# One of the seven products of a gate/up pair made by seven smaller ones over half the tokens

## The chip, the cores and the metric

The kernel runs on one core of one Trainium2 chip. Its time is the device time of one launch in microseconds (us): 1729.62 us before the change, the median of three runs (1728.55 to 1730.23). The matrix engine is TensorE (PE in the profile, PEld its weight loads). VectorE is DVE, ScalarE is ACT, GpSimd is POOL, SyncE is SP; SP issues nearly all the transfers (DMAs). PE accumulates in eight PSUM banks `ps[0]` to `ps[7]`, each of 128 partitions by 512 float32.

## The reference

The input `x` is 64 batches of 64 rows (4096 tokens) by 1024. A small network on `cond_128` gives each batch a 64x64 matrix and a bias, and `y = A x + bias`. Then a feed-forward layer with ternary weights, 1024 to 2752 and back, is added to `x`:

```python
def _bitlinear(x, w):
    scale = jnp.mean(jnp.abs(w))
    q = jnp.round(jnp.clip(w / (scale + EPS), -1.0, 1.0))
    return x @ (q * scale).T

gate = _bitlinear(y, w_gate)
up = _bitlinear(y, w_up)
out = x + _bitlinear(gate * up, w_down)
```

## The kernel before

The tokens go in eight chunks of 512. Chunk 0 quantises and transposes the weights and is computed plainly. Chunks 1 to 7 work on pairs: a pair is two 128-feature tiles of gate and the two of up; there are ten pairs (`NPR`) and half a pair left over (pair 10). Activations are float32 and are split into a float16 high part and a float16 rest, so each weight tile meets two matmuls; weights are fp8.

For each pair the product of a 2x2 block matrix is made by seven products instead of eight (Winograd's form of Strassen's method): the 1024 inputs and the 512 tokens are halved, and so are the four feature tiles of the pair. Products `P1` to `P7` take sums of weight blocks, made once in chunk 0 and kept in device memory (`wcomb`), and sums of activation quarters, made on DVE for each chunk. Each product is 16 matmuls of 128x128 weights by 256 tokens (`product`, L881): two feature tiles (gate and up, side by side in one bank), four inputs tiles, two float16 parts. Gate times up is taken on DVE, and two groups of products (`down_group`, L938) multiply back to 1024, one in the middle of the chunk, after pair 5, and one at its end; DVE adds their results to the output (`output2`, L1762).

Every engine runs its own program in the order in which the code is written; semaphores tie them. In pair `p` PE makes P1, P2, then P4 of the pair before, then (in pairs 2 to 9) one eighth of the next chunk's `y` (`conv`, L658), P6, P5, P3 of the pair before, P7. ACT copies P1 (`copy_p1`, L1241), P1+P6 (`copy_p16`, L1248) and P1+P6+P7 (`copy_p167`, L1255) out of the banks, and in pairs 0 and 1, right behind `copy_p1`, copies the chunk's input to where the output grows (`residual`, L1043, four 128x1024 copies). DVE adds P2, P5 and P3 to those copies (`c11`, `c22`, `c12`), multiplies gate by up (`i11` and so on) and makes the sums of the result.

SP's program for a chunk is one list. `next_x` waits for the chunk's four residual copies, then loads the next chunk's 2 MB of `x` into `xa` and its bias into `bbc`; `pairs` loads each pair's weights from pair 3 on into a ring of three (`ring_load`); `next_pairs` loads the first three pairs of the next chunk, `store2` stores the output, and `down_load` loads the weights of a down group. A step that waits holds back all that stands behind it in the list. From chunk 2 on the chunks run in a loop (`Fori`), the last chunk is written out again.

Of the kernel before, what the change touches and what calls it, by code (L numbers as in the profile page):

```python
# [5 lines left out]
def adaln_ternary_ffn(nc: bass.Bass, x, cond, w0, b0, w1, b1, w2, b2, wk, bias_k, w_gate, w_up, w_down, out):  # L6
# [108 lines left out]
    AFTER = {"P6": "P1", "P7": "P6", "P4": "P7", "P2": "P4", "P3": "P5"}  # L115
    OUT = {"P1": (0, 0), "P2": (0, 0), "P6": (0, 1), "P3": (0, 1), "P4": (2, 0), "P7": (2, 1), "P5": (2, 1), "D": (2, 1)}
    BLOCK = {"P1": 0, "P6": 1, "P5": 2, "P2": 3, "P7": 4, "P4": 5, "P3": 6}

# [41 lines left out]
    with ctx:  # L160
# [27 lines left out]
        scl = bbc  # L188
        raw5 = sb("raw5", [P, CT], f32)

        msk = sb("msk", [P, NM, CT], f8)
# [178 lines left out]
        def wd_block(p, b):  # L370
            at = (p % GRP) * PART + b * BLK
            return wd_flat[:, at:at + BLK]

        psb = [p[:, :].bitcast(bf16) for p in ps]
# [104 lines left out]
        s_wst = [sem("s_wst0"), sem("s_wst1")]  # L479
        s_ring = [sem(f"s_ring{i}") for i in range(RING)]  # L480
        s_turn_pe, s_turn_pool, s_turn_sp = sem("s_turn_pe"), sem("s_turn_pool"), sem("s_turn_sp")
        s_st = [sem(f"s_st{t}") for t in range(NT)]
# [8 lines left out]
        def _(sp):  # L491
# [56 lines left out]
            def ring_load(p):  # L548
# [4 lines left out]
                else:  # L553
                    sp.dma_start(wg_flat[:, at:at + PART].bitcast(f32), wcomb[p, 0]).then_inc(s_ring[p % RING], 16)

            def next_pairs(c):
                for p, before in ((0, NPR - 1), (1, NPR), (2, NPR - 2)):
                    sp.wait_ge(s_m3, NS * (c - FIRST) + before + 1)
                    ring_load(p)

            def down_load(g):
# [3 lines left out]
            def pairs(c):  # L565
                for p in range(RING, NS):
                    sp.wait_ge(s_m3, NS * (c - FIRST) + p - RING + 1)
                    ring_load(p)
# [47 lines left out]
        def _(pool):  # L616
# [28 lines left out]
            for j, i in enumerate(ITEMS):  # L645
# [3 lines left out]
                nc.gpsimd.dma_start(dst, stage(j).bitcast(f32)).then_inc(s_wst[j % 2], 16)  # L649
            chunk(1)  # L650
            with pool.Fori(2, NC - 1) as c:
                chunk(c)
# [3 lines left out]
        def _(pe):  # L656
# [175 lines left out]

            def product(c, p, what):
# [4 lines left out]
                if what == "P1":  # L838
                    pe.wait_ge(s_ring[p % RING], 16 * ((4, 4, 3)[p % RING] * (c - FIRST) + p // RING + 1))
# [31 lines left out]
                elif what == "P3":  # L871
                    pe.wait_ge(s_c22, n + 1)
                if p == 0:
                    pe.wait_ge(s_ylo, KH * c + OPERAND[what] + 1)
                waited(c)
                for h in range(2 if p < NPR else 1):
# [7 lines left out]
                last.then_inc(s_done[what], 1)  # L884

# [17 lines left out]
            def down_group(c, g, more):  # L903
                n, done = NS * (c - FIRST), DN * FIRST + ND2 * (c - FIRST) + g * len(DOWN[0])
                for d, (what, j) in enumerate(DOWN[g]):
                    bank = DBANK[g][CHAIN[what]][j]
                    if d == 0:
                        pe.wait_ge(s_wd, 16 * (2 * (c - FIRST) + g + 1))
                        pe.wait_ge(s_loA, NPR * (c - FIRST) + g * GRP + GRP - 1)
                        pe.wait_ge(s_loS, NPR * (c - FIRST) + g * GRP + GRP - 1)  # L910
                        if g:
                            pe.wait_ge(s_i21, n + NPR)
                    if what in AFTER:
                        pe.wait_ge(s_o, done + DOWN[g].index((AFTER[what], j)) + 1)
                    elif what == "P1" and j:
                        pe.wait_ge(s_c11, n + (NS if g else GRP + 1))
                    elif what == "P5" and g == 0:
                        pe.wait_ge(s_c12 if j else s_i21, n + GRP)
                    elif what == "P5" and j == 0:
                        pe.wait_ge(s_c12, n + NPR)  # L920
                    elif what == "P5":
                        pe.wait_ge(s_uvr, c - FIRST + 1)
                    elif what == "D":
                        pe.wait_ge(s_c12 if j else s_i21, n + NS)
                        if j == 0:
                            pe.wait_ge(s_ulo, UP * FIRST + 2 * (c - FIRST) + 2)
# [64 lines left out]
            def pairs(c, more):  # L991
                for p in range(NS):
                    if p == GRP + 1:
                        down_group(c, 0, more)
                    product(c, p, "P1")
                    product(c, p, "P2")
# [23 lines left out]
        def _(act):  # L1020
# [186 lines left out]
            def hi_quarters(c):  # L1207
                act.wait_ge(s_ysc, KH * c + KH)
                for s in range(8):
                    hi_quarter(c, s)  # L1210

# [57 lines left out]
            def hi_sums(c, p):  # L1269
                act.wait_ge(s_sums, 4 * (NPR * (c - FIRST) + p) + 4)  # L1270
                nc.scalar.copy(pair_parts(p, 0, 3, 4), sums).then_inc(s_hiS, 1)  # L1271

            def hi_rest(c):
                act.wait_ge(s_wr, c - FIRST + 1)
# [5 lines left out]
            def pairs(c, more):  # L1280
                for p in range(NS):
                    copy_p1(c, p)
# [26 lines left out]
        def _(dve):  # L1309
# [291 lines left out]
            def sum_quarter(c, s):  # L1601
# [11 lines left out]
                else:  # L1613
                    dve.wait_ge(s_sy, 4 * (c - FIRST) + 3)
                    dve.wait_ge(s_ylo, KH * c + A12 + 1)
                    V.tensor_tensor(quarter(S4), quarter(A12), quarter(S2), ALU.subtract).then_inc(s_sy, 1)

# [47 lines left out]
            def c11(c, p):  # L1665
# [5 lines left out]
                elif p:  # L1671
                    dve.wait_ge(s_i22, NPR * (c - FIRST) + p)
                elif later(c):
# [15 lines left out]
            def c22(c, p):  # L1689
                n, w = NS * (c - FIRST) + p, width(p)  # L1690
                dve.wait_ge(s_m5, n + 1)
                dve.wait_ge(s_q67, n + 1)
                if p:
                    dve.wait_ge(s_i12, NPR * (c - FIRST) + p)
# [8 lines left out]
            def c12(c, p):  # L1703
                n, w = NS * (c - FIRST) + p, width(p)
                dve.wait_ge(s_m3, n + 1)
                dve.wait_ge(s_q6, n + 1)
                if p < NPR - 1:
                    dve.wait_ge(s_i11, NPR * (c - FIRST) + p + 2)
# [4 lines left out]
            def i12(c, p):  # L1713
                dve.wait_ge(s_c12, NS * (c - FIRST) + p + 1)
                V.scalar_tensor_tensor(a_block(p, A12), rr[:, u], PROD, rr[:, g], ALU.mult, ALU.mult).then_inc(s_i12, 1)  # L1715

            def i21(c, p):
                dve.wait_ge(s_m4, NS * (c - FIRST) + p + 1)
# [3 lines left out]
            def sums3(c, p):  # L1722
                m = NPR * (c - FIRST) + p
                dve.wait_ge(s_i21, NS * (c - FIRST) + p + 1)
                if p or later(c):
                    dve.wait_ge(s_loS, m)
# [38 lines left out]
            def tail(c, more):  # L1765
                lo_a(c, NPR - 1)
                c22(c, NPR)
                lo_s(c, NPR - 1)
                if more:
                    scales(c + 1)  # L1770
                dve.wait_ge(s_gr, c + 1)
# [16 lines left out]
                        (("scale", 6), ("scale", 7)), (("sum", S1), ("lo", A11)), (("lo", A21),), (("sum", S3),), \  # L1788
                        (("sum", S2),), (), (("lo", A12),), (("sum", S4),), (("lo", A22),), (("lo", S1),), (("lo", S2),), \
                        (("lo", S3),), (("lo", S4),)  # L1790
                for d in range(len(DOWN[1])):
                    output2(c, 1, d)
                    if more:
                        for what, k in steps[d]:
                            if what == "scale":
                                scale_y(c + 1, k)
                            elif what == "sum":
                                sum_quarter(c + 1, k)
# [8 lines left out]
            def pairs(c, more):  # L1807
                for p in range(NS):
# [10 lines left out]
                    if p < NPR:  # L1819
                        c11(c, p)  # L1820
# [6 lines left out]
                    if more and p - 2 in range(KH):  # L1827
                        conv(c + 1, p - 2)
                    if p:
                        c12(c, p - 1)  # L1830
                        i12(c, p - 1)
                        sum4(c, p - 1)
                tail(c, more)

# [30 lines left out]
```

## Time and profile before

| | |
|---|---|
| median of three runs | 1729.62 us |
| the profiled execution's own span, first to last instruction | 1726.1 us |
| PE busy, share of the span | 1707.7 us, 99% |
| matmuls of the products (L881) | 8232 |
| matmuls of the down groups (L938) | 1960 |
| DVE, ACT, POOL busy | 63%, 33%, 2% |
| mean granted TensorE clock, share of full speed | 0.999 |

A timeline row has the start and length in us from the span's start. Matmuls are pipelined, so the records of two that follow each other overlap: the pace of PE is read from the distance of starts, not from the length of a record. What an engine waited for stands in brackets behind a row, with the us that it was idle. An engine that is far from full can still hold PE up, if PE waits for one of its steps; how full it is on average doesn't tell that.

### The profile page before, as it was taken

What the parts mean: (1) busy time and instruction counts of PE and PEld (TensorE: products, weight loads), DVE (VectorE), ACT (ScalarE), POOL (GpSimd) and SP (SyncE); (2) the same over time, 40 slices, a digit from 0 to 9 for tenths busy, and PEclk for the clock granted to TensorE, in tenths of its full rate; (3) what the DMA queues carried; (4) which work ended last, traced back from release to release, by engine and by line L of the source; (5) the groups of instructions that cost most, each with busy time, mean ns of one, the idle gap of its engine ahead of it and who ended that gap; (6) DMA issues with size and microseconds to landing.
All of it is one profiled execution on the core that took longest, in us unless ns stands there. A gap on an engine that the chain in (4) does not pass through costs nothing.

```text
span 1726.1 us, 31355 instructions
## 1 busy us (share of the span) xinstructions
PE 1707.7 (99%) x12424; PEld 1215.6 (70%) x12424; DVE 1096.0 (63%) x1786; ACT 575.6 (33%) x921; POOL 28.0 (2%) x59
## 2 busy tenths in 40 slices
PE   6999999999999999999999999999999999999999
PEld 5554545968769596795958768596776959678684
DVE  6898895555766468554685646755576545855464
ACT  6887732312333133230333213231233313323120
POOL 0010000000000000000000000000000000000000
PEclk9999999999999999999999999999999999999999
DMA  8666626312242032420224211331223313132021
GB/s 342 249 229 239 221 96 219 121 44 97 76 148 96 22 108 77 168 66 22 107 102 164 65 75 54 129 137 43 97 76 126 101 40 108 65 124 79 29 87 49
DMA packets 59735, 194.06 MB, mean 112 GB/s; under 512 B 5280, under 2 KB 5600, under 8 KB 59584
## 3 DMA queue, kind: packets, MB, share of 16 engines
q1 hardware_dynamic: 56432, 177.49, 28.9%
q0 software_dynamic: 2560, 14.36, 2.2%
q8 instruction: 109, 1.79, 0.4%
q14 instruction: 42, 0.34, 0.1%
q10 hardware_dynamic: 592, 0.09, 0.0%
HBM read 160.90 MB, written 31.01 MB: 111 GB/s over the span
## 4 chain that ended last, share of the span: by engine, by line
PE 97%; DVE 2%; DMA 1%; issue 0%; ACT 0%; SPq 0%; DVEq 0%
PE ps L881 52%; PE ps L938 25%; PE ps L658 17%; PE ps L899 2%; PE ps L761 1%; DMA xa<-in_x_dram 1%; DVE wsum L1318 0%; DVE ys L1413 0%; DVE msk L1458 0%; DVE ys L1380 0%; DVE xa L1529 0%; DVE prod L1496 0%; DVE yp L1418 0%; ACT wdT L1106 0%; SPq L493 0%
## 5 line engine op out<-in xcount | busy, mean ns | idle before, releaser
L881 PE MATMUL ps<-yp,wgT 128*128 128x256 f16 x4116 | 902.4, 273 | 1.1 <-issue 1.1
L881 PE MATMUL ps<-wuT,wgT 128*128 128x256 f16 x4116 | 902.4, 273 | 0.0
L881 PEld LDWEIGHTS ps<-yp,wgT 128*128 128x128 fp8e4 x4116 | 402.9, 98 | 50.8 <-issue 2.9
L881 PEld LDWEIGHTS ps<-wuT,wgT 128*128 128x128 fp8e4 x4116 | 402.7, 98 | 48.3
L938 PE MATMUL ps<-wdT,inter 128*128 128x512 fp8e4 x1960 | 433.2, 379 | 0.0
L938 PEld LDWEIGHTS ps<-wdT,inter 128*128 128x128 f16 x1960 | 191.1, 98 | 227.2 <-issue 1.4
L1762 DVE SCALAR_TENSOR_TENSOR xr<-ps,osc,xr 128x512 f32<-128x512 f32 x210 | 156.4, 748 | 168.2 <-PE ps L938 128.4
L1711 DVE TENSOR_TENSOR wdT<-ps,msk 128x512 f32<-128x512 f32 (+1 forms) x77 | 51.3, 666 | 207.1 <-PE ps L881 207.1
L1241 ACT COPY raw<-ps 128x512 f32<-128x512 f32 (+1 forms) x77 | 43.7, 567 | 314.6 <-PE ps L881 314.0
L1248 ACT COPY msk<-ps 128x512 f32<-128x512 f32 (+1 forms) x77 | 43.6, 567 | 138.1 <-PE ps L881 138.1
L1263 ACT COPY inter<-ps 128x256 f32<-128x256 f32 x70 | 26.1, 372 | 180.1 <-PE ps L881 180.1
L1745 DVE TENSOR_TENSOR inter<-inter 128x1024 f16<-128x1024 f32 x70 | 85.3, 1218 | 0.0
L1205 ACT CAST yp<-ys 128x1024 f16<-128x1024 f32 x49 | 48.5, 1042 | 102.0 <-DVE ys L1413 59.0
L1675 DVE TENSOR_TENSOR wdT<-ps,raw 128x512 f32<-128x512 f32 x70 | 48.4, 692 | 43.7 <-PE ps L881 43.1
L658 PE MATMUL ps<-yp,wgT 128*128 128x512 f16 x336 | 76.1, 379 | 0.0
L658 PE MATMUL ps<-yp,wuT 128*128 128x512 f16 x336 | 75.1, 379 | 0.0
L658 PE MATMUL ps<-wdT,inter 128*128 128x512 fp8e4 x336 | 73.8, 379 | 0.0
L1267 ACT CAST inter<-prod 128x768 f16<-128x768 f32 x35 | 29.1, 832 | 132.7 <-DVE prod L1715 132.7
L1271 ACT CAST inter<-inter 128x1024 f16<-128x1024 f32 x70 | 73.3, 1047 | 0.0
L1267 ACT CAST inter<-wuT 128x768 f16<-128x768 f32 x35 | 29.1, 832 | 127.7 <-DVE wuT L1715 127.7
L1697 DVE TENSOR_TENSOR wdT<-ps,raw 128x512 f32<-128x512 f32 (+1 forms) x77 | 50.8, 660 | 32.4 <-ACT raw L1255 32.4
L658 PE MATMUL ps<-ablk,xa 128*128 128x128 f32 x512 | 69.5, 282 | 0.6 <-DMA xa<-in_x_dram 0.3
(229 smaller groups left out, 1497.9 us busy)
## 6 DMA issues: line engine op xcount, KB each, us to landing
wgT<-wcomb SPq DMA_DIRECT2D x70, 896.0 KB, 4.7
wdT<-dcomb SPq DMA_DIRECT2D x14, 2240.0 KB, 10.9
xa<-in_x_dram SPq DMA_DIRECT2D x8, 2048.0 KB, 7.8
out_dram<-xr SPq DMA_DIRECT2D x64, 256.0 KB, 2.0
wcomb<-xa POOLq DMA_DIRECT2D x17, 448.0 KB, 3.0
xr<-in_L_ffn_w_down_dram SPq DMA_DIRECT2D x9, 512.0 KB, 5.5
inter<-in_L_ffn_w_gate_dram SPq DMA_DIRECT2D x7, 512.0 KB, 16.6
wdT<-in_L_ffn_w_up_dram SPq DMA_DIRECT2D x7, 512.0 KB, 4.4
```

What stands on the lines that cost most here:

```text
L658: return nc.tensor.matmul(o, l, r, start=start, stop=stop)
L881: last = nc.tensor.matmul(out, w, operand(i, OPERAND[what])[:, k, :], start=(start and h + k + i == 0), stop=(k == KQ - 1 and i == 1), ski ...
L938: last = nc.tensor.matmul(bank[:, :], x, wd_block(p, BLOCK[what]), start=(what in ("P1", "P2", "P5") and q + i == 0), stop=(q == GRP - 1 a ...
L1205: nc.scalar.copy(operand(0, s), quarter(s)).then_inc(s_yhi, 1)
L1241: nc.scalar.copy(t1[:, 0:w], PB[p % 2][:, 0:w]).then_inc(s_t1, 1)
L1267: nc.scalar.copy(pair_parts(p, 0, 0, 3), blocks4[p % 2][:, HALF:4 * HALF]).then_inc(s_hiA, 1)
L1271: nc.scalar.copy(pair_parts(p, 0, 3, 4), sums).then_inc(s_hiS, 1)
L1675: V.tensor_tensor(rr if p < NPR else g21, PA[:, 0:w], t1[:, 0:w], ALU.add).then_inc(s_c11, 1)
L1697: V.tensor_tensor(rr[:, TOK - w:TOK], PC[p % 2][:, 0:w], q67[:, 0:w], ALU.add).then_inc(s_c22, 1)
L1711: V.tensor_tensor(rr[:, 0:w], PC[p % 2][:, 0:w], q6[p % 2][:, 0:w], ALU.add).then_inc(s_c12, 1)
L1745: V.tensor_tensor(pair_parts(p, 1, 3, 4), sums, pair_parts(p, 0, 3, 4), ALU.subtract).then_inc(s_loS, 1)
L1762: V.scalar_tensor_tensor(xr[:, t, cols], bank[:, :], osc[:, t:t + 1], xr[:, t, cols], ALU.mult, ALU.add).then_inc(s_o, 1)
```

## The change

In chunks 2 to 7 and pairs 0 to 9, product P2 is itself made by seven products. Its 512 inputs are halved and its 256 tokens too (128 and 128); the two feature tiles, gate and up, are the third halving. Each inner product is 4 matmuls of 128 tokens (two input tiles, two float16 parts), 28 in place of 16 matmuls of 256 tokens.

- The four sums of weight blocks that this needs are made in chunk 1 by POOL, pair by pair from the ring, and stored to `wsub` (128 KB a pair). SP loads those of a pair into one of two buffers, `hi_r` for even pairs and `sub1` for odd ones. The load for pair `p - 1` stands ahead of the ring load of pair `p`, so that for pair 2 stands behind `next_x`. The load of the second down group's weights moves from pair 8 to pair 10 of the list.
- The four sums of activation quarters are made on DVE at the end of the chunk before (`inner_sums`, four additions or subtractions of 128x256), split by ACT (`hi_inner`) and DVE (`inner_lo`), both 128x1024.
- PE makes the seven in four places of a pair: two behind P1 (`inner_a`), one behind P4 (`inner_b`), one in the middle of P6 (`inner_g`), three ahead of P7 (`inner_d`). `inner_a` waits for the weight sums.
- Between them ACT copies 128-token pieces from bank 5 (`inner1`, `inner2`, `inner3`: four copies of 128x128), and DVE adds once (`inner_upper`).
- ACT's residual copies of pairs 0 and 1 move from behind `copy_p1` to behind `copy_p16`. On DVE, `c11` and `i11` of a pair move behind the pair's other work, and some of the waits between such steps are changed to fit.

The first place is ACT in pair 1 of the loop's chunks. Before (`raw` and `msk` are the copies of P1 to P7's banks, `inter<-ps` is P4's gate part):

```order
L1241 COPY raw<-ps 128x512
L1043 COPY xr<-xa 128x1024 x2
L1263 COPY inter<-ps 128x256
L1248 COPY msk<-ps 128x512
L1266 ISA
```

And now, from `copy_p1` of pair 1 on:

```order
L1375 COPY raw<-ps 128x512
L1408 REGISTER_ALU
L1409 COPY ps<-ps 128x128
L1397 COPY inter<-ps 128x256
L1413 COPY wuT<-ps 128x128
L1417 COPY wuT<-ps 128x128
L1418 COPY ps<-ps 128x128
L1382 COPY msk<-ps 128x512
L1175 COPY xr<-xa 128x1024 x2
```

The pair's residual copies (`xr<-xa`) stood second and now stand last, behind the copy of P1+P6 and all that PE makes up to there.

The second place is SP at the start of a chunk in the loop. Before, with the semaphores that each row waits for:

```order
L543 ISA [waits s_xr]
L496 ISA [waits s_y]
L496 DMA xa<-in_x_dram 128x4x1024
L506 ISA [waits s_ysc]
L506 DMA bbc<-biasd 128x512
L567 ISA
L552 DMA wgT<-wcomb 128x2x896 [waits s_m3]
```

And now (`s_xr` counts the residual copies, `s_m2` the finished P2, `s_m3` the finished P3):

```order
L569 ISA [waits s_xr]
L522 ISA [waits s_y]
L522 DMA xa<-in_x_dram 128x4x1024
L532 ISA [waits s_ysc]
L532 DMA bbc<-biasd 128x512
L606 ISA
L584 DMA hi_r<-wsub 128x256 [waits s_m2]
L578 DMA wgT<-wcomb 128x2x896 [waits s_m3]
```

The new row, the weight sums of pair 2, stands directly behind the loads of `x` and of the bias.

The core of the diff:

```diff
+    INNER, TH = "P2", P
+        wsub = nc.dram_tensor("wsub", [NPR, P, HALF], f32).ap()
+            def sub_load(p):
+                dst = (hi_r[:, :].bitcast(f32), sub1[:, :].bitcast(f32))[p % 2]
+                sp.dma_start(dst, wsub[p]).then_inc(s_sub[p % 2], 16)
...
             def next_pairs(c):
+                if isinstance(c, int) and c == FIRST:
+                    sp.wait_ge(s_subd, NPR)
                 for p, before in ((0, NPR - 1), (1, NPR), (2, NPR - 2)):
                     sp.wait_ge(s_m3, NS * (c - FIRST) + before + 1)
                     ring_load(p)
...
+                sub_load(1)
+                sp.wait_ge(s_ulo, UP * FIRST + 2 * (c - FIRST) + 1)
+                sub_load(0)
             def pairs(c):
                 for p in range(RING, NS):
+                    if not (isinstance(c, int) and c == FIRST):
+                        sp.wait_ge(s_m2, NS * (c - FIRST) + p - 2)
+                        sub_load(p - 1)
                     sp.wait_ge(s_m3, NS * (c - FIRST) + p - RING + 1)
+                    if isinstance(c, int) and c == FIRST:
+                        sp.wait_ge(s_subd, p - RING + 1)
                     ring_load(p)
-                    if p == 8:
+                    if p == NPR:
...
+            for p in range(NPR):
+                pool.wait_ge(s_ring[p % RING], 16 * (p // RING + 1))
+                nc.gpsimd.tensor_tensor(st[:, 0], uk[0], gk[0], ALU.subtract, saturate=False).then_inc(s_subt, 1)
...
+                nc.gpsimd.dma_start(wsub[p], p2[:, (p % 2) * HALF:(p % 2 + 1) * HALF]).then_inc(s_subw[p % 2], 16)
...
+            def inner(p, out, x, w, start=False):
+                for k in range(2):
+                    for i in range(2):
+                        last = nc.tensor.matmul(out, w[k], inner_x(i, x)[:, k, :], start=(start and k + i == 0),
+                                                stop=(k + i == 2), skip_group_check=True)
+                return last
+            def inner_a(c, p):
+                pe.wait_ge(s_sub[p % 2], 16 * (NPR // 2 * (c - FIRST - 1) + p // 2 + 1))
...
+                inner(p, IB[:, 0:TH], IA11, quarter_w(p, 0, 0), True)
+                inner(p, IB[:, TH:2 * TH], IS1, inner_sum_w(p, 0)).then_inc(s_ia, 1)
+            def inner_b(c, p):
+                pe.wait_ge(s_e1, NPR * (c - FIRST - 1) + p + 1)
+                inner(p, IB[:, 0:TH], IS2, inner_sum_w(p, 1)).then_inc(s_ib, 1)
+            def inner_g(c, p):
+                pe.wait_ge(s_e2, NPR * (c - FIRST - 1) + p + 1)
+                inner(p, IB[:, 0:TH], IS3, inner_sum_w(p, 2)).then_inc(s_ig, 1)
+            def inner_d(c, p):
+                pe.wait_ge(s_ir, NPR * (c - FIRST - 1) + p + 1)
+                inner(p, PA[:, 0:TH], IA12, quarter_w(p, 0, 1))
+                inner(p, PA[:, 2 * TH:3 * TH], IS4, quarter_w(p, 1, 1))
+                inner(p, PA[:, TH:2 * TH], IA22, inner_sum_w(p, 3)).then_inc(s_m2, 1)
...
+                    if p < NPR and not (isinstance(c, int) and c == FIRST):
+                        product(c, p, "P1")
+                        inner_a(c, p)
+                        if p:
+                            product(c, p - 1, "P4")
+                        else:
+                            product(c, p, "P5", 0)
+                        inner_b(c, p)
+                        if more and p - 2 in range(KH):
+                            conv(c + 1, p - 2)
+                        product(c, p, "P6", 0)
+                        inner_g(c, p)
+                        product(c, p, "P6", 1)
+                        product(c, p, "P5", None if p else 1)
+                        if p:
+                            product(c, p - 1, "P3")
+                        inner_d(c, p)
+                        product(c, p, "P7")
+                        continue
...
+            def inner1(c, p):
+                nc.scalar.copy(PA[:, 0:TH], IB[:, 0:TH]).then_inc(s_e1, 1)
+            def inner2(c, p):
+                nc.scalar.copy(upper[:, 0:TH], IB[:, 0:TH]).then_inc(s_e2, 1)
+            def inner3(c, p):
+                nc.scalar.copy(upper[:, TH:2 * TH], IB[:, 0:TH])
+                nc.scalar.copy(PA[:, TH:2 * TH], IB[:, 0:TH]).then_inc(s_e3, 1)
...
                     copy_p1(c, p)
-                    if p < 2:
+                    if split:
+                        inner1(c, p)
+                    if p < 2 and not split:
                         residual(c, 2 * p)
                         residual(c, 2 * p + 1)
                     if p:
                         gate21(c, p - 1)
+                    if split:
+                        inner2(c, p)
+                        inner3(c, p)
                     copy_p16(c, p)
+                    if p < 2 and split:
+                        residual(c, 2 * p)
+                        residual(c, 2 * p + 1)
...
+            def inner_upper(c, p):
+                dve.wait_ge(s_e3, NPR * (c - FIRST - 1) + p + 1)
+                V.tensor_tensor(PA[:, HALF:TOK].rearrange("p (a n) -> p a n", a=2),
+                                upper.rearrange("p (a n) -> p a n", a=2),
+                                IB[:, TH:2 * TH].unsqueeze(1).broadcast_to([P, 2, TH]), ALU.add).then_inc(s_ir, 1)
```

## Rows read from the trace of the kernel before

**Rows 1.** The page's first line, and part 4: the chain's shares by engine.

```profile
span 1726.1 us, 31355 instructions
...
PE 97%; DVE 2%; DMA 1%; issue 0%; ACT 0%; SPq 0%; DVEq 0%
```

**Rows 2.** The chain in time, start of chunk 3: start us, us, what, matmuls.

```profile
703.51 26.36 PE ps L881 x240
730.76 12.23 PE ps L881 x112
```

**Rows 3.** Timeline of PE, chunk 0: start us, us, engine, line, what.

```profile
62.86 0.61 PE L761 MATMUL ps<-identb,msk 128*128 128x128 bf16 x8
63.31 3.62 PE L658 MATMUL ps<-yp,wgT 128*128 128x512 f16 x16
```

**Rows 4.** Timeline, the weight loads of the next such burst.

```profile
66.55 0.65 PEld L761 LDWEIGHTS ps<-identb,msk 128*128 128x128 bf16 x8
```

**Rows 5.** Part 5 of the page, weight loads of the products: busy, mean ns, idle.

```profile
L881 PEld LDWEIGHTS ps<-yp,wgT 128*128 128x128 fp8e4 x4116 | 402.9, 98 | 50.8 <-issue 2.9
```

**Rows 6.** Timeline of ACT, pair 1 of chunk 3.

```profile
714.18 0.59 ACT L1241 COPY raw<-ps 128x512 f32<-128x512 f32 x1 [1.16 <-PE ps L881]
714.67 1.99 ACT L1043 COPY xr<-xa 128x1024 f32<-128x1024 f32 x2
```

**Rows 7.** Timeline of SP's queue, the same stretch.

```profile
716.96 0.40 SPq L496 DMA_DIRECT2D xa<-in_x_dram  x1
717.57 0.35 SPq L506 DMA_DIRECT2D bbc<-biasd  x1
```

**Rows 8.** Waits of SP's queue: us in total, times, longest.

```profile
SPq L543 <- ACT xr L1043: 54.7, 5, 11.2
```

**Rows 9.** Transfers by line: count, KB each, median us from issue to landing.

```profile
xa<-in_x_dram SPq DMA_DIRECT2D x8, 2048.0 KB, 7.8
out_dram<-xr SPq DMA_DIRECT2D x64, 256.0 KB, 2.0
...
bbc<-biasd SPq DMA_DIRECT2D x7, 256.0 KB, 7.9
```

**Rows 10.** Timeline, the first `conv` of the next chunk in pair 2 of chunk 3.

```profile
729.70 1.06 PE L658 MATMUL ps<-ablk,xa 128*128 128x128 f32 x8
```

**Rows 11.** Groups of ACT by shape: copies out of PSUM.

```profile
L1263 ACT COPY inter<-ps 128x256 f32<-128x256 f32 x70 | 26.1, 372 | 180.1 <-PE ps L881 180.1
...
L1112 ACT ACTIVATE wdT<-ps 64x128 fp8e4<-64x128 fp8e4 x16 | 4.3, 266 | 0.1
```

**Rows 12.** Timeline of DVE, a later pair of chunk 3.

```profile
818.82 0.69 DVE L1711 TENSOR_TENSOR wdT<-ps,msk 128x512 f32<-128x512 f32 x1 [3.25 <-PE ps L881]
...
820.10 0.42 DVE L1736 TENSOR_TENSOR inter<-wuT,inter 128x256 f32<-128x256 f32 x1
```

**Rows 13.** Timeline of DVE, last output of chunk 2's second down group.

```profile
703.22 0.75 DVE L1762 SCALAR_TENSOR_TENSOR xr<-ps,osc,xr 128x512 f32<-128x512 f32 x1 [0.92 <-PE ps L899]
```

**Rows 14.** Stretches: us, PE busy (matmuls), granted clock, DMA share, GB/s.

```profile
28.00:29.00 1.00, 0.30 (x5) 0.82 1.02 406
29.00:30.00 1.00, 1.00 (x5) 0.50 1.01 401
30.00:31.00 1.00, 1.00 (x7) 0.50 1.03 414
31.00:32.00 1.00, 1.00 (x6) 0.50 1.04 418
32.00:33.00 1.00, 1.00 (x11) 0.97 1.02 406
```

**Rows 15.** Timeline of PE, two idle spells of chunk 0.

```profile
28.70 0.26 PE L658 MATMUL ps<-onesb,l 1*128 1x1 bf16 x4 [2.03 <-DVE l L1409]
...
36.72 1.72 PE L658 MATMUL ps<-inter 128*64 128x448 f32 x8 [3.16 <-ACT msk L1061]
```

**Rows 16.** Groups of POOL by shape: busy, mean ns.

```profile
L270 POOL COPY ablk<-aT 64x256 f32 x10 | 5.9, 594 | 976.1 <-PE ps L658 974.9 <-POOL ablk L270 1.3
```

More of the change, by code:

```diff
@@ L116, in adaln_ternary_ffn @@
     OUT = {"P1": (0, 0), "P2": (0, 0), "P6": (0, 1), "P3": (0, 1), "P4": (2, 0), "P7": (2, 1), "P5": (2, 1), "D": (2, 1)}
+    INNER, TH = "P2", P
+    IA11, IA12, IS1, IS2, IS3, IS4, IA22 = range(7)
     BLOCK = {"P1": 0, "P6": 1, "P5": 2, "P2": 3, "P7": 4, "P4": 5, "P3": 6}
@@ L372, in wd_block, with inner_x, inner_w @@
             return wd_flat[:, at:at + BLK]
+        IB, isums = ps[5], sums.rearrange("p (s k n) -> p s k n", s=4, k=2)
+        upper = wu_flat[:, 4 * KH * TOK + 8 * TOK:4 * KH * TOK + 10 * TOK].bitcast(f32)
+        sub_hl = [b[:, :].bitcast(f16).rearrange("p (s k n) -> p s k n", s=4, k=2) for b in (p2, g_r)]
+        sub_w = [b.rearrange("p (s k n) -> p s k n", s=4, k=2) for b in (hi_r[:, :].bitcast(f8), sub1[:, :])]
+        sub_stage = [p2[:, i * HALF:(i + 1) * HALF].bitcast(f8).rearrange("p (s k n) -> p s k n", s=4, k=2)
+                     for i in range(2)]
+        def inner_x(i, s):
+            if s in (IA11, IA12, IA22):
+                k, t = {IA11: (0, 0), IA12: (2, 0), IA22: (2, TH)}[s]
+                return operand(i, OPERAND[INNER])[:, k:k + 2, t:t + TH]
+            return sub_hl[i][:, s - IS1]
+        def inner_w(p, h, kh, k):
+            return ring(p, h, BLOCK[INNER], 2 * kh + k)
         psb = [p[:, :].bitcast(bf16) for p in ps]
@@ L831, in down, with product @@
                 last.then_inc(s_dn, 1)
-            def product(c, p, what):
+            def product(c, p, what, half=None):
                 n = NS * (c - FIRST) + p
@@ L837, in product @@
                 bank = PA if what == "P2" else (PC if what in ("P5", "P3") else PB)[p % 2]
-                if what == "P1":
+                if half == 1:
+                    pass
+                elif what == "P1":
                     pe.wait_ge(s_ring[p % RING], 16 * ((4, 4, 3)[p % RING] * (c - FIRST) + p // RING + 1))
@@ L872, in product @@
                     pe.wait_ge(s_c22, n + 1)
-                if p == 0:
+                if p == 0 and half != 1:
                     pe.wait_ge(s_ylo, KH * c + OPERAND[what] + 1)
-                waited(c)
-                for h in range(2 if p < NPR else 1):
+                if half != 1:
+                    waited(c)
+                for h in range(2 if p < NPR else 1) if half is None else (half,):
                     out = bank[:, h * HALF:(h + 1) * HALF]
@@ L912, in down_group @@
                             pe.wait_ge(s_i21, n + NPR)
+                        elif not (isinstance(c, int) and c == FIRST):
+                            pe.wait_ge(s_ir, NPR * (c - FIRST - 1) + GRP + 1)
                     if what in AFTER:
@@ L1281, in pairs @@
                 for p in range(NS):
+                    split = p < NPR and not (isinstance(c, int) and c == FIRST)
                     copy_p1(c, p)
-                    if p < 2:
+                    if split:
+                        inner1(c, p)
+                    if p < 2 and not split:
                         residual(c, 2 * p)
@@ L1615, in sum_quarter @@
                     dve.wait_ge(s_ylo, KH * c + A12 + 1)
+                    if not (isinstance(c, int) and c == FIRST):
+                        dve.wait_ge(s_isum, 4 * (c - FIRST))
                     V.tensor_tensor(quarter(S4), quarter(A12), quarter(S2), ALU.subtract).then_inc(s_sy, 1)
@@ L1671, in c11 @@
                 elif p:
-                    dve.wait_ge(s_i22, NPR * (c - FIRST) + p)
+                    dve.wait_ge(s_i12 if later(c) else s_i22, NPR * (c - FIRST) + p)
                 elif later(c):
@@ L1692, in c22 @@
                 dve.wait_ge(s_q67, n + 1)
-                if p:
+                if later(c) and p < NPR:
+                    dve.wait_ge(s_i11, NPR * (c - FIRST) + p + 1)
+                elif p:
                     dve.wait_ge(s_i12, NPR * (c - FIRST) + p)
@@ L1706, in c12 @@
                 dve.wait_ge(s_q6, n + 1)
-                if p < NPR - 1:
+                if later(c) and p < NPR:
+                    dve.wait_ge(s_i22, NPR * (c - FIRST) + p + 1)
+                elif p < NPR - 1:
                     dve.wait_ge(s_i11, NPR * (c - FIRST) + p + 2)
@@ L1724, in sums3 @@
                 dve.wait_ge(s_i21, NS * (c - FIRST) + p + 1)
+                if p == 0 and later(c):
+                    dve.wait_ge(s_ilo, c - FIRST)
                 if p or later(c):
@@ L1769, in tail @@
                 if more:
+                    if not later(c):
+                        for i in range(2):
+                            dve.wait_ge(s_subw[i], 16 * (NPR // 2))
                     scales(c + 1)
@@ L1788, in tail @@
                         (("scale", 6), ("scale", 7)), (("sum", S1), ("lo", A11)), (("lo", A21),), (("sum", S3),), \
-                        (("sum", S2),), (), (("lo", A12),), (("sum", S4),), (("lo", A22),), (("lo", S1),), (("lo", S2),), \
-                        (("lo", S3),), (("lo", S4),)
+                        (("sum", S2),), (("inner", 0),), (("lo", A12),), (("sum", S4),), (("lo", A22),), (("lo", S1),), \
+                        (("lo", S2),), (("lo", S3), ("inner", 1)), (("lo", S4),)
                 for d in range(len(DOWN[1])):
@@ L1796, in tail @@
                                 scale_y(c + 1, k)
+                            elif what == "inner":
+                                (inner_sums, inner_lo)[k](c + 1)
                             elif what == "sum":
@@ L1818, in pairs @@
                             output2(c, 0, d)
-                    if p < NPR:
+                    if p < NPR and not later(c):
                         c11(c, p)
@@ L1828, in pairs @@
                         conv(c + 1, p - 2)
+                    if p < NPR and later(c):
+                        inner_upper(c, p)
                     if p:
@@ L1832, in pairs @@
                         sum4(c, p - 1)
+                    if p < NPR and later(c):
+                        c11(c, p)
+                        i11(c, p)
                 tail(c, more)
```

70 lines of the change are left out of this document (69 added, 1 removed).

## The prediction

> **What bounds the kernel now.** First the page: PE holds 97% of the chain that ends last [rows 1], so what PE does and waits for is the time. Next the chain in time, for the pace. 112 matmuls of the products take 12.23 us [rows 2], 0.1092 us each for 256 tokens; a product of 16 takes 1.747 us. The first two pairs of a chunk are 240 matmuls in 26.36 us, at the same pace [rows 2], so PE waits for nothing inside the pairs. Then the timelines of ACT, DVE and SP, to see how much room their steps have before PE asks for their result; that is where a change in the order can cost.
>
> **What the inner products save on PE.** 16 matmuls of 256 tokens become 28 of 128 in ten pairs of six chunks, 60 times. No product here runs over 128 tokens. The nearest row is a burst of transposes: eight 128x128 bf16 matmuls start at 62.86, and the next group starts at 63.31 [rows 3], so 0.45 / 8 = 0.0563 us each, each with weights of its own. A weight load is recorded with 98 ns [rows 5], but eight of them fit into 0.65 us in such a burst [rows 4], so the records overlap. From below I bound the pace by half of 0.1092, 0.0546 us; from above by one load after the other, 0.098 us, which the burst speaks against. I take 0.0563: it is the same width with the same load in front. Then 28 x 0.0563 = 1.575 us against 1.747, 0.172 us less, and 60 x 0.172 = 10.3 us less on PE. The ends give 60 x (1.747 - 28 x 0.0546) = 13.1 us less and 60 x (2.744 - 1.747) = 59.8 us more.
>
> The burst's pace has a rule against it. The Trainium skill (TensorE: Matmul & The Clock Gate, Back-to-back issue gap) gives about 81 ns a matmul for 128 columns in a sustained stream of loads and matmuls, and calls 56 ns the isolated gap. Here eight in a row kept 56 ns, so the trace speaks against the rule as far as a burst can. By the rule the saving would turn into a loss: 28 x 0.081 = 2.27 us against 1.747 a pair.
>
> **The steps between the inner products.** I lay a pair out from its start, with the durations above. P1 ends at 1.75, `inner_a` at 2.20, P4 at 3.94, `inner_b` at 4.17, `conv` (0.89, from 729.87 to 730.76 in [rows 2]) at 5.06, half of P6 at 5.93, `inner_g` at 6.16, the rest of P6 at 7.03, P5 and P3 at 10.53, `inner_d` at 11.20, P7 at 12.95. The new ACT copies are 128x128. Their price lies between 0.27 us, a small copy out of PSUM, and 0.37 us, the copy of 128x256 [rows 11]; I take 0.27 for the first. `inner1` waits for `copy_p1` (0.59) and is done near 2.6; `inner_b` wants it at 3.94. `inner2` stands behind the copy of P4's gate part (0.37) and is done near 4.6; `inner_g` wants it at 5.93, or at 5.04 where no `conv` stands between. The two copies of `inner3` are done near 6.7, and `inner_upper` on DVE (128x256, 0.42 as such an addition takes [rows 12]) near 7.4; `inner_d` wants it at 10.53. DVE has this time, since it now waits 3.25 us for P3 in each pair [rows 12]. So they cost nothing. Without this cover, at 0.37 us a copy, the tightest one would still be in time by some 0.3 us.
>
> The c11 and i11 that move on DVE follow P3's steps and fill a wait for ACT there. The rest of the change on DVE and ACT is at a chunk's end: four sums (0.42 each) and one split of 128x1024, some 2.9 us. DVE has five spells of about 0.9 us there, the last of them ahead of 703.22 [rows 13]; the additions eat about half of them, and PE does not wait. POOL's 40 additions in chunk 1 are on no row; at the 0.59 us of its copy of 64x256 [rows 16] they are 2.4 us a pair, and up to twice that if the width counts, against 13 us that PE spends on a pair. I take nothing for them, with 1 us of doubt to each side.
>
> **What is moved past SP's queue.** This is the step that decides. SP's list for a chunk begins with a wait for the four residual copies, and the trace shows that it really waits there for ACT, five times [rows 8]: in chunk 3 the second pair of copies begins 0.49 us after the start of the copy before and takes 1.99 us, to 716.66 [rows 6]; the load of x is issued at 716.96, 13.45 us after the chunk's start at 703.51, and the bias 0.61 us later [rows 2, 7]. Now the copies stand behind P6 of pair 1. Pair 0 is four whole products and the seven inner ones, 4 x 1.747 + 1.575 = 8.56 us. P6 of pair 1 ends 1.747 + 0.45 + 1.747 + 0.225 + 0.874 + 0.225 + 0.874 = 6.14 us later, at 14.70. With 0.03 for the signal, 0.49 and 1.99 the residual copies end at 17.2, and the load of x is issued at 17.5, four us later than before.
>
> It lands 7.8 us later, at 25.3. The first `conv` wants it in pair 2. Pair 2 starts at 8.56 + 12.06 = 20.6, and its `conv` is due 4.17 later, at 24.8 (before: at 26.2, from 729.70 [rows 10], with 5 us to spare). That alone would be a stall of 0.5 us.
>
> The sums of pair 2 are worse off. They are due when P1 of pair 2 ends, at 20.6 + 1.75 = 22.4. SP issues their load behind those of x and the bias, at about 18.6. On this queue a transfer waits for those ahead: the bias, 256 KB, lands 7.9 us after its issue, where 256 KB stored alone take 2.0 us [rows 9]; it lands 0.7 us after x, in front of which it can't get. The 128 KB of sums come behind both. With half of the bias's 0.7 they land near 18.1 + 7.9 + 0.35 = 26.4. PE stands still from 22.4 to 26.4: 4.0 us. The delay of `conv` falls inside this.
>
> This happens in each chunk that loads a next one and has inner products, 2 to 6, five times: 5 x 4.0 = 20.1 us. In chunk 7 SP has no x to load, and pairs 0 and 1 got their sums at the end of the chunk before. From pair 3 on the sums are queued behind one ring load, and PE is 4 us later, so nothing else is late. Bounds: at least 25.3 - 22.4 = 2.9 us a chunk if the sums land with x, about 5 us if they share the queue with the ring load of pair 3, which is issued right behind.
>
> **The clock behind such a gap.** The granted clock fell from its upper level (2.4 GHz) to 0.50 (1.2 GHz) near 28.6, after PE had stood idle for 2.03 us and had been mostly idle for some us ahead of that; it came back near 32 [rows 14, 15]. That stretch gave up 0.18 + 3 x 0.50 + 0.03 = 1.7 us. After another idle time, 3.16 us ahead of 36.72, I saw no fall [rows 15]. A gap of 4.0 us behind full work lies above both. Between no fall and five falls (0 to 8.5 us) I take three, 5.1 us. The Trainium skill (TensorE: Matmul & The Clock Gate, HAM oscillation) says that a wait for a transfer in every tile throttles each tile anew. By it all five would fall; the second idle time above disagrees, the first agrees.
>
> **The sum.** 1726.1 - 10.3 + 20.1 + 5.1 = 1741.0 us of span. The median of the runs, 1729.6, lies 3.5 us above the span of the profiled execution, which I add: 1744.5, and I say 1744 us, slower by 0.8%. Without a fall of the clock it is 1739.4, with five 1747.9.
>
> **Rivals.**
> 1. *The sums do not wait behind x.* If transfers of one queue overtake each other, the 128 KB land within some 2 us, ahead of 22.4, and `conv` alone waits 0.5 us for x in five chunks: 1729.6 - 10.3 + 2.5 = 1722 us, faster. The turn is at 2.1 us a chunk, 10.3 / 5. For it: nothing on this queue; against it: the bias. 9%.
> 2. *Weight loads bound the inner products.* At the recorded 98 ns of a load they take 59.8 us more than P2 did, and with the stalls and the clock the time is 1729.6 + 59.8 + 25.2 = 1815. For it: the length of the load's record, and that no burst in the trace goes on for 12 matmuls; against it: the overlapping records of the burst. 6%. By the Trainium skill's 81 ns (TensorE: Matmul & The Clock Gate, Back-to-back issue gap) it would be 31 us more than P2, and about 1786.
> 3. *The copies between the inner products come late.* If each of 60 pairs lost 0.2 us to ACT or to PE's own start after a wait, the saving is gone: about 1756 us. For it: four more waits a pair; against it: the spare times above, 0.5 us at the least. 5%.
> 4. *The stall is half as long*, because x lands sooner with less beside it: 1729.6 - 10.3 + 5 x 2 = 1729, no change. 4%.
>
> My forecast, a stall of 3 to 5 us in five chunks with none to five falls of the clock, has 76%. Its own range is 1734 to 1753: 2.9 us without a fall gives 1734, 5 us with five falls 1753. I give 1733 to 1755, which lets in part of rival 3. Within 0.2% (3.5 us) a measurement of this kernel can't tell from no change: same is 1726.2 to 1733.1. Slower: 76 + 6 + 5 - 1 = 86%; same: rival 4 and the lower edge, 5%; faster: rival 1, 9%.
>
> **What would show it.** In the profile after: PE idle for some 4 us ahead of `inner_a` of pair 2 in chunks 2 to 6, released by the transfer of `wsub`, and nowhere else; the x load issued some 17.5 us after a chunk's start, bound to land 25 us after it; a pair from pair 3 on that takes 12.95 us instead of 13.1 with its `conv`; 128-token matmuls 56 ns apart; stretches of clock 0.5 behind some of the gaps. I am wrong about the path if the gap is short or absent, about the pace if a pair without a gap is no shorter than before.

## The result and the profile after

The changed kernel takes 1756.22 us (median of 4 runs, 1755.9 to 1757.7) against 1729.09 (1728.27 to 1730.23). The ratio is 1.0162, 95% interval 1.0149 to 1.0174: slower by 1.6%. The forecast was 1744, with a range of 1733 to 1755; the direction and the place of the loss were right, its size was not: 27 us where 14 were foreseen.

The page after: the span, the busy time of the engines, and the chain that ended last by engine. It answers to [rows 1].

```profile
span 1754.5 us, 33623 instructions
PE 1709.3 (97%) x13136; PEld 1223.2 (70%) x13144; DVE 1126.6 (64%) x1876; ACT 635.4 (36%) x1167; POOL 62.8 (4%) x109
PE 94%; DMA 4%; SPq 1%; DVE 1%; issue 0%; ACT 0%; DVEq 0%
```

The span grew by 28.4 us, and a transfer now has 4% of the chain. The view of waits on PE says which (columns: line, releaser, us in total, times, longest):

```profile
PE ps L955 <- DMA hi_r<-wsub: 27.6, 5, 5.9
```

Five waits for the weight sums, 27.6 us. They are nearly all of the growth, so what else has changed must nearly cancel. First the gap of chunk 2, whose P1 starts at 498.10. SP's issues there, after (start, us, what):

```profile
515.76 0.42 SPq L522 DMA_DIRECT2D xa<-in_x_dram  x1
516.37 0.36 SPq L532 DMA_DIRECT2D bbc<-biasd  x1
516.86 0.34 SPq L584 DMA_DIRECT2D hi_r<-wsub  x1
517.25 0.50 SPq L578 DMA_DIRECT2D wgT<-wcomb  x1
```

The load of x goes out 17.66 us after the chunk's start, where [rows 2, 7] had 13.45. The chain in time shows what that does (start, us, what; short pieces left out):

```profile
512.08 4.37 PE ps L946 x40
...
516.86 9.02 DMA hi_r<-wsub
...
527.02 3.11 PE ps L946 x16
```

128 KB take 9.02 us with 2 MB of x and the bias ahead of them on the queue; issued ahead of x ("the sums first", below), they take 3.6 to 6.1. PE's own timeline around the gap (in brackets the idle time ahead and its releaser):

```profile
520.34 0.27 PE L946 MATMUL ps<-wuT,wgT 128*128 128x256 f16 x1
...
526.01 0.26 PE L955 MATMUL ps<-yp,wgT 128*128 128x128 f16 x1 [5.41 <-DMA hi_r<-wsub]
...
526.82 0.42 PE L946 MATMUL ps<-yp,wgT 128*128 128x256 f16 x1
...
529.97 0.22 PE L955 MATMUL ps<-p,hi_r 128*128 128x128 f16 x1
```

PE stops at 520.45, 22.3 us after the chunk's start, and goes on at 526.01. The eight matmuls of `inner_a` then take 0.81 us, not 0.45, and the 16 of P4 3.15, not 1.75: near half speed. The stretches show the clock (us, PE busy, PEld, DVE, ACT, POOL, then PEclk, DMA share, GB/s):

```profile
521.00:523.50 2.50, 0.00 (x0) 0.00 (x0) 1.30 (x2) 0.23 (x1) 0.00 (x0) 0.87 1.04 333
523.50:526.00 2.50, 0.00 (x0) 0.02 (x1) 0.00 (x0) 0.00 (x0) 0.00 (x0) 0.50 0.98 309
526.00:527.00 1.00, 0.99 (x9) 0.97 (x10) 0.00 (x0) 0.00 (x0) 0.00 (x0) 0.50 1.01 407
527.00:528.00 1.00, 1.00 (x7) 0.70 (x5) 0.00 (x0) 0.25 (x1) 0.00 (x0) 0.50 0.32 112
528.00:529.00 1.00, 1.00 (x7) 0.67 (x6) 0.00 (x0) 0.00 (x0) 0.00 (x0) 0.50 0.00 0
529.00:530.00 1.00, 1.00 (x8) 0.76 (x7) 0.00 (x0) 0.00 (x0) 0.00 (x0) 0.66 0.00 0
530.00:531.00 1.00, 1.00 (x13) 1.00 (x11) 0.36 (x1) 0.54 (x2) 0.00 (x0) 1.00 0.00 0
```

The clock falls from 2.4 to 1.2 GHz while PE stands still, and PE pays for it once it works again: 0.36 + 1.40 = 1.76 us behind this gap. In chunks 2 to 6 it takes 3.95, 4.03, 3.89, 4.06 and 4.22 us from the restart to `inner_b` (`inner_a` and P4), where 2.20 are needed at the upper level: 1.7 to 2.0 us each, 9.2 in all. Other than in [rows 14, 15], PE had been at full work ahead of it.

Now the inner products themselves, on PE's timeline:

```profile
504.24 0.22 PE L955 MATMUL ps<-yp,wgT 128*128 128x128 f16 x1
504.29 0.22 PE L955 MATMUL ps<-wuT,wgT 128*128 128x128 f16 x1
...
504.85 0.22 PE L955 MATMUL ps<-wuT,hi_r 128*128 128x128 f16 x1
504.91 0.27 PE L946 MATMUL ps<-yp,wgT 128*128 128x256 f16 x1
```

`inner_d`, twelve matmuls, goes from 504.24 to 504.91: 0.67 / 12 = 0.0558 us each. The other inner products hold the same pace, so the seven take 0.447 + 0.223 + 0.223 + 0.670 = 1.563 us where P2 took 1.747. Chunk 7, which loads no x and makes no `conv`, shows this by itself: from its P1 to the end of the span it took 200.97 us before and takes 199.15 now, 1.82 less for ten pairs.

The last term was not foreseen. `conv` now comes behind matmuls of 128 tokens:

```profile
556.12 0.22 PE L955 MATMUL ps<-g_r,hi_r 128*128 128x128 f16 x1
556.17 1.11 PE L720 MATMUL ps<-ablk,xa 128*128 128x128 f32 x8
557.12 0.27 PE L946 MATMUL ps<-yp,wgT 128*128 128x256 f16 x1
```

It takes 0.95 us, from 556.17 to 557.12, where it took 0.89; all 40 took 35.7 us before and take 37.9 now.

| Term | foreseen, us | in the trace after, us |
|---|---|---|
| inner products in place of P2, 60 times | -10.3 | 60 x (1.563 - 1.747) = -11.0 |
| gap ahead of `inner_a` of pair 2, five times | +20.1 | 27.6 + 5 x 0.16 = +28.4 |
| clock at half behind the gap | 3 x 1.7 = +5.1 | +9.2 |
| `conv` behind 128 tokens, 40 times | 0 | 37.9 - 35.7 = +2.1 |
| sum | +14.9 | +28.7 |
| span | | +28.4 |

The 0.16 us is the tail of the record ahead of each gap. The last matmul of P1 has a record of 0.27 us where PE's pace is 0.109 (520.34 to 520.61), and the view counts PE as idle only from the record's end. The rows come to 0.3 us more than the span grew.

### The profile page after: what moved, and what is told of

It reads as the page before. It is cut to its first block, busy times and chain, and to the rows that moved or that the text cites. A ratio compares the mean times of both kernels' runs of the same rounds, so it can differ in the third digit from the quotient of the medians.

```text
span 1754.5 us, 33623 instructions
## 1 busy us (share of the span) xinstructions
PE 1709.3 (97%) x13136; PEld 1223.2 (70%) x13144; DVE 1126.6 (64%) x1876; ACT 635.4 (36%) x1167; POOL 62.8 (4%) x109
## 4 chain that ended last, share of the span: by engine, by line
PE 94%; DMA 4%; SPq 1%; DVE 1%; issue 0%; ACT 0%; DVEq 0%
PE ps L946 45%; PE ps L1051 24%; PE ps L720 17%; PE ps L955 5%; DMA hi_r<-wsub 3%; PE ps L1010 2%; SPq L551 1%; DMA wuT<-in_L_ffn_w_gate_dram 1%; PE ps L823 1%; DVE msk L1619 0%; DVE xa L1690 0%; DVE prod L1657 0%; ACT wdT L1238 0%; SPq L519 0%; DVE xa L1693 0%
## 5 line engine op out<-in xcount | busy, mean ns | idle before, releaser
L946 PE MATMUL ps<-yp,wgT 128*128 128x256 f16 x3636 | 815.5, 274 | 0.5 <-issue 0.2
L946 PE MATMUL ps<-wuT,wgT 128*128 128x256 f16 x3636 | 815.1, 274 | 0.0
L946 PEld LDWEIGHTS ps<-yp,wgT 128*128 128x128 fp8e4 x3636 | 357.8, 98 | 44.4 <-issue 2.4
L946 PEld LDWEIGHTS ps<-wuT,wgT 128*128 128x128 fp8e4 x3636 | 357.6, 98 | 42.4
L1911 DVE SCALAR_TENSOR_TENSOR wuT<-ps,inter 128x256 f32<-128x256 f32 x35 | 14.9, 424 | 85.5 <-ACT inter L1397 85.5
L955 PE MATMUL ps<-yp,wgT 128*128 128x128 f16 x240 | 40.4, 222 | 27.6 <-DMA hi_r<-wsub 27.6
L720 PEld LDWEIGHTS ps<-ablk,xa 128*128 128x128 f32 x512 | 64.0, 196 | 2.6 <-DVE ys L1541 1.1
```

Of the source, the lines that this page charges most:

```text
L720: return nc.tensor.matmul(o, l, r, start=start, stop=stop)
L955: last = nc.tensor.matmul(out, w[k], inner_x(i, x)[:, k, :], start=(start and k + i == 0), stop=(k + i == 2), skip_group_check=True)
```

## Experiments

The profile leaves two things open. Is the gap made by the residual copies, which hold up x, or by the sums' place behind x? And why did the transfers take longer than foreseen? All ratios are to the kernel before, on the same chip.

**The residual copies early again.** The inner products stay; the copies return to about where they stood.

```diff
+ if p == 1 and split: residual(c, 3)                    # behind inner1
- if p < 2 and split: residual(c, 2*p); residual(c, 2*p+1)   # behind the late copy
+ if p == 0 and split: residual(c, 0); residual(c, 1)    # behind copy_p16
+ if p == 0 and split: residual(c, 2)                    # behind copy_p167
```

> The change, with the four residual copies put where ACT has room: two behind copy_p16 of pair 0, one behind copy_p167 of pair 0, one behind inner1 of pair 1. SP's list is as in the change. Theory A (the late x load in front of pair 2's sums is the whole loss): x is issued about 12.7 us after a chunk's start in place of 17.7, the sums land near 22.0 to 22.8 against 22.4 where PE asks, so the gap falls from 5.6 us to 0.5 or less and the clock stays up: 1756 - 5 x 7.3 = about 1720 us. Theory B (the inner products and their waits themselves cost most of the loss): the gap goes but the time stays above 1740. Theory C (place in the list is what counts, however early x goes): the gap stays above 3 us, time above 1740.

1718.79 us (1718.45 to 1720.76), ratio 0.9947 (0.9934 to 0.9961): faster than before by 0.5%. SP issues x 12.5 us after the chunk's start (500.00 here):

```profile
512.51 0.42 SPq L522 DMA_DIRECT2D xa<-in_x_dram  x1
513.12 0.36 SPq L532 DMA_DIRECT2D bbc<-biasd  x1
513.62 0.34 SPq L584 DMA_DIRECT2D hi_r<-wsub  x1
```

The sums still stand behind x and the bias, PE does not wait for them, and the granted clock has a mean of 0.997 where it had 0.988. So theory A of the text above holds: the place of the copies made the gaps and the falls of the clock. Without them the inner products show their gain.

**The sums first.** The copies stay late; SP takes the sums of pair 2 ahead of x.

```diff
+ def first_sums(c):
+     sp.wait_ge(s_m2, NS * (c - FIRST) + 1)
+     sub_load(RING - 1)          # at the head of SP's list for the chunk
  ...
- if not (c == FIRST):
+ if not (c == FIRST or p == RING):     # not again in the pairs
```

> The change, with pair 2's weight sums issued at the head of SP's list, ahead of the wait for the residual copies and of the x load; the copies stay late. Theory A: the gap ahead of inner_a of pair 2 is gone, and what stays is conv of pair 2, due 24.8 us after the chunk's start with x landing at 25.5 to 26.5: 0.7 to 1.8 us a chunk, five times, no or few falls of the clock; about 1724 to 1729 us. Theory B: above 1740.

1729.64 us (1728.0 to 1733.76), ratio 1.0009 (1.0 to 1.0018). SP's issues, and PE's waits for x in the view of waits:

```profile
507.03 0.33 SPq L584 DMA_DIRECT2D hi_r<-wsub  x1
...
517.68 0.41 SPq L522 DMA_DIRECT2D xa<-in_x_dram  x1
```

```profile
PE ps L728 <- DMA xa<-in_x_dram: 8.6, 5, 2.0
```

The sums cost nothing any more; `conv` waits 1.7 us for x in five chunks, and no clock falls behind these waits (mean 0.997, as with the early copies). That is A again, 0.6 us above its range: a late x alone eats the gain of the inner products, the sums behind it make the loss.

**Both.**

> Both of the last two edits. Theory A: no gap at all; what is left is the saving of the inner products, 1.747 - 1.56 = 0.187 us in 60 pairs less 0.06 us in 40 pairs where conv behind 128-token matmuls takes 0.95 in place of 0.89: 8.8 us, so 1729.1 - 8.8 = 1720 us, and the same as or up to 3 us below the run with early copies. Theory B: not below 1729.

1719.03 us (1718.4 to 1720.46), ratio 0.9947 (0.9934 to 0.9961), the same as the early copies alone. With x early, the order of sums and x on the queue is worth nothing.

**Late copies alone.** The kernel before, P2 whole, with the copies put as late as the change puts them.

```diff
+ split = p < NPR and not (isinstance(c, int) and c == FIRST)
- if p < 2:
+ if p < 2 and not split:
      residual(c, 2*p); residual(c, 2*p+1)
  copy_p16 ...
+ if p < 2 and split:
+     residual(c, 2*p); residual(c, 2*p+1)
```

> The kernel before, with the residual copies of pairs 0 and 1 behind copy_p16 in chunks 2 to 7 and nothing else of the change: no inner products and no weight sums. x is then issued near 18.5 us after a chunk's start and lands 7.8 to 8.9 us later, at 26.3 to 27.4, where conv is due at 26.2. Theory A (the loss needs both, x late and the sums behind it): a gap of 0.1 to 1.2 us in five chunks ahead of conv, 1728.5 to 1734 us, and no fall of the clock. Rival: the late copies alone make the loss, 1740 or more.

1729.8 us (1728.67 to 1732.82), ratio 1.001 (1.0001 to 1.002). x is issued as late (516.50 in chunk 2, 18.7 us after the chunk's start), and PE waits for it by this much (0.7 of it in chunk 0, 0.1 to 0.2 in each chunk of the loop):

```profile
PE ps L658 <- DMA xa<-in_x_dram: 1.3, 4, 0.7
```

So neither part makes the 27 us alone: the late copies need the sums queued behind x, and the sums behind x need the late copies. In the changed kernel the late copies still cost the whole gain, 1729.64 (sums first) against 1719.03 (both); in the kernel before they cost 0.1%, since `conv` is due 1.4 us later there (26.2 us after the chunk's start, 24.8 in the changed kernel).

**Why the transfers take longer: sharing?** In the kernel after, the list of transfers says (KB each, median us to landing):

```profile
xa<-in_x_dram SPq DMA_DIRECT2D x8, 2048.0 KB, 9.0
bbc<-biasd SPq DMA_DIRECT2D x7, 256.0 KB, 9.2
hi_r<-wsub SPq DMA_DIRECT2D x30, 128.0 KB, 4.8
```

In chunks 2 to 6 x lands 8.8 to 9.2 us after its issue, where it took 7.6 to 7.8 before (median 7.8 in [rows 9]). Suspect one is the ring load of pair 3, 896 KB right behind the sums. Here SP holds it until the sums are in:

```diff
+ if p == RING and not (isinstance(c, int) and c == FIRST):
+     sp.wait_ge(s_sub[0], 16 * (NPR // 2 * (c - FIRST - 1) + 2))
  ring_load(p)
```

> The change, with one more wait on SP: pair 3's ring load (896 KB) is issued only after pair 2's sums have landed. It tells why the gap is 5.6 us and not the 4.0 that I had worked out. Theory S (what is queued behind shares the engines with what is ahead): x lands after about 7.8 us in place of 8.8, the sums 1 to 1.3 us sooner, gap about 4.4 us, time 5 to 9 us below the change. Theory T (the sums' small rows or the bias are slow in themselves): landing times and gap stay, time as the change within 2 us.

1757.71 us, ratio 1.0168 (1.0153 to 1.0184). SP's issues and PE's wait:

```profile
517.48 0.34 SPq L584 DMA_DIRECT2D hi_r<-wsub  x1
526.28 0.38 SPq L578 DMA_DIRECT2D wgT<-wcomb  x1
```

```profile
PE ps L957 <- DMA hi_r<-wsub: 25.8, 5, 5.4
```

With nothing queued behind the sums x still takes 8.8 to 9.1 us, and the gap shrinks from 5.5 to 5.2. Theory S, the sharing, falls; of the growth it holds 0.4 us a chunk at most. The numbers are those of theory T, but not for its reason: x itself, which stands ahead of the bias and the sums, is what takes longer.

**Why the transfers take longer: an instruction fetch?** The queues in the stretch 517 to 524.6 of the kernel after (queue, kind: packets, MB, share of 16 engines):

```profile
q1 hardware_dynamic: 737, 2.41, 95.8%
q8 instruction: 1, 0.02, 0.8%
```

One packet of instructions goes over one of the 16 transfer engines while x does; its 0.8% of 16 engines in 7.6 us is 1.0 us of one. By the 16 signals that tell of x's landing, 15 of its shares land between 522.86 and 523.48, and one at 524.55. In the kernel before all 16 land within 0.44 us (518.56 to 519.00), and no such packet is in the stretch. The fetch falls some 5 us behind the x issue. That it is the late share's engine that has the fetch isn't in the trace. If the fetch is the cause, an x issued still later, behind the fetch, must land in under 8 us again. So with the sums first, x waits for P4 of pair 1:

```diff
- sp.wait_ge(s_xr, NT * c)
- sp.wait_ge(s_y, KH * c + KH)
+ sp.wait_ge(s_m4, NS * (c - FIRST) + 2)     # in chunks past FIRST
```

> Sums first, and the x load held back until P4 of pair 1 is done, about 24.9 us after the chunk's start, to see what makes x land 8.8 to 9.2 us after its issue in the change and 7.4 to 7.8 where it goes early. Theory F (an instruction fetch, 16 KB on one of the 16 transfer engines, comes near 23.7 us after the chunk's start and holds back that engine's share of x by about 1.1 us): x now starts behind the fetch and lands after 7.4 to 7.8 us. Theory L (x is slower the later it is issued in the chunk, or the more is queued behind it): 8.8 or more. Either way PE waits for conv, 7.5 to 9 us in five chunks, and the time is near 1765 us.

One run: 1771.3 us, 6 above what was expected, with the clock lower behind each of the five gaps (mean 0.984); PE now waits for x itself.

```profile
PE ps L731 <- DMA xa<-in_x_dram: 39.0, 6, 7.9
```

x goes out at 522.93, lands 7.5 to 7.8 us later in all five chunks, and its stretch (524 to 531) has no instruction packet:

```profile
q1 hardware_dynamic: 626, 2.30, 96.8%
```

What theory F forecast came true, though the fetch had moved too: it comes 19.9 us after the chunk's start here, 5 us ahead of x. Over the eight other kernels of this study the same split shows in chunks 2 to 6. The fifteen x loads with a fetch some 5 us in (after, sums first, ring held) took 8.7 to 9.2 us, each with one share late and the other fifteen in by 7.8. The five of late copies alone, whose fetch comes 0.1 to 0.8 us after x has landed, took 7.6 to 7.8; of the others all but one took 7.4 to 7.8. That one, of the last kernel below, took 8.7 us with no fetch beside it; there all 16 shares are late, and I can't explain it.

Late copies alone also speaks against theory L: x goes out later there (18.7 us after the chunk's start, 17.7 in the change), the fetch comes later still (26.5 to 27.2, where it was 22.8 to 23.2), and x is quick. And the kernel before has the case itself, in chunk 1, which the change leaves as it was (stretch 306 to 315):

```profile
q8 instruction: 1, 0.02, 0.7%
...
xa<-in_x_dram SPq DMA_DIRECT2D x1, 2048.0 KB, 9.0
```

In all nine kernels this load has a fetch 4.7 to 5.1 us in, takes 8.8 to 9.2 us and has one late share. So 24 loads of 24 with a fetch in their middle were late. No run moved the fetch and left all else as it was, so F rests on where fetch and x stood.

**`conv` ahead of `inner_b`.** On top of "both", `conv` now follows P4's matmuls of 256 tokens.

```diff
+ conv(...)
  inner_b(c, p)
- conv(...)
```

> Early copies and sums first, and PE makes the eighth of the next chunk's y (conv) ahead of inner_b in place of behind it. In the change conv takes 0.95 us behind inner_b against 0.89 behind P4 before. Theory W (its first float32 weight load can't hide behind a matmul of 128 tokens): conv takes 0.89 again and 8 x 5 x 0.06 = 2.4 us are saved, 1719.0 - 2.4 = 1716.6 us. Rival V (the 0.06 us goes over to inner_b, whose load then stands behind conv): time stays at 1719 within 1 us.

1717.61 us (1716.44 to 1719.59), ratio 0.9939 (0.9926 to 0.9953). PE's timeline:

```profile
550.75 1.06 PE L728 MATMUL ps<-ablk,xa 128*128 128x128 f32 x8
551.64 0.22 PE L963 MATMUL ps<-p,hi_r 128*128 128x128 f16 x1
```

`conv` is back at 0.89 us (550.75 to 551.64) and `inner_b` stays at 0.22, so theory W's number comes true and rival V falls: what stands ahead of `conv` sets its price. W's reason, the weight load, is not shown. The span falls from 1718.7 to 1717.1, 1.6 us where 2.4 were expected; by the times alone this version and "both" can't be told apart. It has the lowest median here, 0.6% below the kernel before.

## Why the prediction was right and wrong

- **PE bounds the kernel, and only its waits count.** Right: apart from the five gaps nothing PE waits for has changed by more than 0.7 us in all.
- **The saving.** Right in kind and near in size: 11.0 us for 10.3. Runs of 4, 8 and 12 matmuls all hold the 56 ns that was read from a burst of eight [rows 3]. Rival 2 falls, and with it the rule of the Trainium skill (TensorE: Matmul & The Clock Gate, Back-to-back issue gap) for 128 columns, as far as bursts of twelve go: 81 ns were stated, 55.8 measured.
- **The copies between the inner products** cost nothing, as argued: the five waits for the sums are the only ones in the view of waits on the line of the inner products. Rival 3 falls; that its 1756 us is the measured time is chance. POOL's additions, taken at nothing, cost nothing: chunk 1 lasts 205.10 us before and 205.09 after.
- **SP's list decides.** Right, place and releaser: x issued 17.66 us after the chunk's start (17.5 foreseen), PE stopping at 22.3 (22.4), the sums behind x and the bias, five times, `conv` hidden inside the gap. Rivals 1 and 4 fall.
- **"It lands 7.8 us later, at 25.3": this step failed.** It lands 8.8 us later in chunk 2 (8.8 to 9.2 in the five chunks), at 26.5. At its new place an instruction fetch falls into the transfer, and where one did, x was late each time. I took the duration of x from its old place, and the bounds of the gap, 2.9 to 5 us, allowed for company behind the sums, not for a longer x; the 9.0 us of chunk 1's x in the kernel before were a sign of it. The sums landed at 27.8, 1.4 us past the 26.4 that was foreseen; 1.0 of that is x's longer transfer, 0.16 its later issue, and the rest, 0.2, fits the 0.4 us that holding the ring load gave back. Five times some 1.5 us are the 7.5 us by which the gap term was short.
- **The clock was the other mis-sized term.** "I take three" of five falls; all five came, at 1.7 to 2.0 us each for 1.7: 9.2 us for 5.1, 4.1 us more. The sentence of the Trainium skill beside it (TensorE: Matmul & The Clock Gate, HAM oscillation: a wait for a transfer in every tile throttles every tile) agrees with five of five here. The gaps of up to 2.0 us with the sums first had no such stretch behind them.
- **`conv`** was taken at its old 0.89 us behind a new neighbour: 2.1 us, on no line of the prediction. That what stands ahead of it is the cause is shown by moving it.

## What to carry to other kernels

Moving an instruction on one engine moves every transfer whose issue waits for it, and everything queued behind that: price a small load by the large one ahead of it, and give it a place where it need not wait. A transfer's duration was measured at one place; when it moves, look at what else is on the queues at the new place, instruction fetches among it. Where PE will stand still for some 5 us, add the slow clock behind the gap to every one of them: here it came each time.

## What the runs showed of the hardware

- One instruction packet of 0.02 MB in the middle of a 2 MB load went with a late sixteenth of it: 8.7 to 9.2 us in place of 7.4 to 7.8, in 24 loads of 24 (fifteen in the loop, nine in chunk 1).
- 128 KB on SP's queue behind 2 MB and 256 KB took 9.0 us in chunk 2, and 3.6 to 6.1 when issued ahead of them; [rows 9] had 2.0 us for a store of 256 KB alone.
- Behind gaps of 5.1 to 7.9 us after full work the granted clock was at its lower level (1.2 GHz) in 15 cases of 15 (the change, the ring held, x later still); behind gaps of 1.6 to 2.0 us in none of five (sums first).
- Eight float32 matmuls of `conv` took 0.95 us behind a 128-column matmul and 0.89 behind a 256-column one. Why is open; no run measured it by itself.
